# Second attention: the scores of four heads as one job of four 32-row tiles, in place of two jobs of two heads

## What is computed

```python
q = (x @ wq).reshape(b, s, 32, 8).transpose(0, 2, 1, 3)      # b = 2, s = 1024
k = (x @ wk).reshape(b, s, 8, 8).transpose(0, 2, 1, 3)
v = (x @ wv).reshape(b, s, 8, 8).transpose(0, 2, 1, 3)
q, k = rope(q), rope(k)
k, v = repeat(k, 4, axis=1), repeat(v, 4, axis=1)
scores = einsum('bhqd,bhkd->bhqk', q, k) / 8 ** 0.5
scores = where(causal, scores, -inf)
out = einsum('bhqk,bhkd->bhqd', softmax(scores), v)
x = x + layernorm(out.transpose(0, 2, 1, 3).reshape(b, s, 256) @ wo)
```

## Time and profile before

| | |
|---|---|
| median of 3 runs | 1905.16 us (1902.91 to 1907.54) |
| the profiled execution | 1904.82 us, its span 1903.1 us |
| TensorE, VectorE, ScalarE, GpSimd busy | 87%, 73%, 59%, 35% of the span |
| second attention, unit 0's first score job to the end of unit 15 | 1214.1 to 1700.7 us |
| mean granted clock of TensorE | 0.948 of full speed |

### The profile page before, as it was taken

How to read it: one execution, slowest core, us unless ns; L and a number is a source line. 1 busy time by engine, 2 the same in 40 slices (tenths; PEclk the granted TensorE clock), 3 DMA queues, 4 the chain that set the end, 5 groups by cost and what they waited for, 6 DMA issues and landing times. The chain is left out here.

```text
span 1903.1 us, 43770 instructions
## 1 busy us (share of the span) xinstructions
PE 1654.3 (87%) x14612; PEld 1020.7 (54%) x14612; DVE 1383.8 (73%) x2882; ACT 1129.0 (59%) x2158; POOL 667.5 (35%) x756
## 2 busy tenths in 40 slices
PE   3899999999999999999827745899999999982997
PEld 1577777777777777777713422233333333341554
DVE  4487777778777777777766564888888888837564
ACT  4566666666666666666545641266666666666444
POOL 0654554555455555545221123021212222223011
PEclk9899999999999999999968967899999999995998
DMA  4322111112111111211000010000000000001000
GB/s 130 88 54 49 41 47 43 43 41 52 47 41 47 44 41 41 52 47 34 17 0 1 1 36 9 17 13 15 15 13 16 12 18 11 8 1 66 1 23 22
DMA packets 53107, 61.83 MB, mean 32 GB/s; under 512 B 11345, under 2 KB 32018, under 8 KB 53010
## 3 DMA queue, kind: packets, MB, share of 16 engines
q1 hardware_dynamic: 53010, 60.55, 13.1%
HBM read 18.57 MB, written 2.10 MB: 11 GB/s over the span
## 5 line engine op out<-in xcount | busy, mean ns | idle before, releaser
L1566 ACT ACTIVATE a_prob<-psum 128x1024 f32<-128x1024 f32 (+3 forms) x384 | 302.3, 813 | 212.1 <-PE psum L1523 209.5
L1606 DVE TENSOR_REDUCE a_mx<-psum 128x1 f32<-128x512 f32 (+3 forms) x608 | 367.5, 655 | 61.2 <-PE psum L1505 55.0
L1598 POOL TENSOR_SCALAR_AFFINE_SELECT a_prob<-a_prob 128x256 f32<-128x256 f32 x256 | 103.8, 406 | 420.5 <-ACT a_prob L1566 418.0
L1502 PE MATMUL psum<-a_kd,a_qp 128*128 128x512 f16 (+3 forms) x768 | 217.5, 337 | 34.2 <-DMA a_kd<-a_k_part 22.6
L528 POOL TENSOR_TENSOR a_swp<-a_swp,a_sin 128x512 f32<-128x512 f32 x128 | 163.1, 1274 | 161.6 <-DMA a_swp<-a_lin 161.6
L884 DVE TENSOR_REDUCE a_nmax<-psum 128x1 f32<-128x1024 f32 (+7 forms) x256 | 191.3, 748 | 1.0 <-PE psum L599 1.0
L532 POOL TENSOR_TENSOR a_rope<-a_swp,a_cosd 128x512 f32<-128x512 f32 x128 | 164.2, 1283 | 12.4 <-POOL a_swp L528 4.7
L224 POOL TENSOR_TENSOR x<-x,y (+1 forms) x64 | 54.4, 879 | 319.5 <-ACT y L196 319.5
L1544 PE MATMUL psum<-a_prob,a_vg 128*32 128x512 f32 (+3 forms) x1536 | 165.4, 503 | 0.8 <-ACT a_o_sb L1572 0.4
L1502 PEld LDWEIGHTS psum<-a_kd,a_qp 128*128 128x128 f16 x768 | 70.7, 98 | 173.3 <-DVE a_mx L1606 94.4
L756 ACT ACTIVATE a_prob_big<-psum,a_nmax 128x1024 f32<-128x1024 f32 (+3 forms) x128 | 121.8, 952 | 68.5 <-DVE a_nmax L884 65.1
(11 more groups left out here) (256 smaller groups left out, 4477.8 us busy)
## 6 DMA issues: line engine op xcount, KB each, us to landing
a_swp<-a_lin SPq DMA_DIRECT2D x256, 128.0 KB, 2.3
a_qp<-a_q_part SPq DMA_DIRECT2D x192, 16.0 KB
a_kd<-a_k_part SPq DMA_DIRECT2D x192, 16.0 KB
x<-_attn_hidden_states_dram SPq DMA_DIRECT2D x4, 512.0 KB, 5.5
a_w_raw<-in_L_attn_Wq_dram SPq DMA_DIRECT2D x16, 128.0 KB, 2.3
a_w_raw<-in_L_attn_Wk_dram SPq DMA_DIRECT2D x16, 128.0 KB, 2.3
a_w_raw<-in_L_attn_Wv_dram SPq DMA_DIRECT2D x16, 128.0 KB, 2.3
a_wo_raw<-in_L_attn_Wo_dram SPq DMA_DIRECT2D x1, 2048.0 KB
```

What stands on the lines that cost most here:

```text
L1502: last = pe.matmul(to[:, j * n:(j + 1) * n], qp[:, w % 3, t * P:(t + 1) * P], kd[:, w % 3, j0 + j, a:e], start=True, stop=not edge)
L1566: act.activation(prob_at(u, i)[:, 2 * pair:2 * pair + 2, a % BANK:a % BANK + e - a], c.psum[:, pair_of(u, i):pair_of(u, i) + 2, 0:e - a], ...
L1606: dve.tensor_reduce(mx[:, t, j0:j0 + per, a // BANK], work(("S", w, i))[:, 0:per * (e - a)].rearrange("p (j n) -> p j n", j=per), AX.X, AL ...
```

## The change

A place is one score job of four heads. Its four matmuls go to four different 32-row tiles and to banks 0, 1, 2 and 3; the exponential is one instruction over four banks, up to 2048 columns; the mask is one instruction over four heads. Since there are no other four banks, a score job waits for the exponential of the job just before it. The context of a place stands directly behind the next score job. Score jobs are due at 2i + 1. ScalarE's copy of bank 4 stands one place after the half's last context place (at place 4 and at place 0 of the next unit). Scans, maxima, outputs, and VectorE's work keep their numbers and due times.

```diff
@@ the places and the order
-                KQ += [(t, max(t * P, half * BANK), (half + 1) * BANK, pair) for pair in range(2)]
-        NS, NJ, NC = len(QK), len(KQ), len(KQ) // 2
+                KQ.append((t, max(t * P, half * BANK), (half + 1) * BANK))
+        NS, NC = len(QK), len(KQ)
-            timed = [(i + 0.5, "X", i) for i in range(NJ)] if u >= 0 else []
+            timed = [(2 * i + 1, "X", i) for i in range(NC)] if u >= 0 else []
-                timed += [(2 * LAST_OF[0] + 1 + LAG + 2.6, "O", 0)]
+                timed += [(2 * LAST_OF[0] + 5.6, "O", 0)]
@@ TensorE
-                        wait(pe, exp_done, NJ * u + i - 1)
+                        wait(pe, exp_done, NC * u + i)
                         pe.wait_ge(qf_ready, 2 * u + a // BANK + 1)
-                        for h in range(2):
-                            rows = slice((2 * pair + h) * R, (2 * pair + h + 1) * R)
-                            last = pe.matmul(c.psum[:, pair_of(u, i) + h, 0:e - a], kd[rows, u % 3, 2 * pair + h, kt * P:(kt + 1) * P],
+                        for j in range(J):
+                            rows = slice(j * R, (j + 1) * R)
+                            last = pe.matmul(c.psum[:, j, 0:e - a], kd[rows, u % 3, j, kt * P:(kt + 1) * P],
                                              qf[rows, u % 2, a:e], start=True, stop=True)
@@ the context behind a score job
-                            done = NJ * u + i - LAG
-                            if done >= 0 and done % 2 == 1:
-                                context(done // NJ, done % NJ // 2)
+                            if NC * u + i >= 1:
+                                context(*divmod(NC * u + i - 1, NC))
@@ ScalarE
-                        act.activation(prob_at(u, i)[:, 2 * pair:2 * pair + 2, a % BANK:a % BANK + e - a],
-                                       c.psum[:, pair_of(u, i):pair_of(u, i) + 2, 0:e - a], ACT.Exp, scale=SCALE).then_inc(exp_done, 1)
+                        act.activation(prob_at(u, i)[:, :, a % BANK:a % BANK + e - a],
+                                       c.psum[:, 0:J, 0:e - a], ACT.Exp, scale=SCALE).then_inc(exp_done, 1)
-                            if i == 2 * LAST_OF[0] + 1 + LAG:
+                            if i == LAST_OF[0] + 1:
                                 output(u, 0)
-                            if i == LAG - 1 and u >= 1:
+                            if i == 0 and u >= 1:
                                 output(u - 1, 1)
@@ GpSimd
-                                block_ = prob_at(u, i)[:, 2 * pair:2 * pair + 2, a % BANK:a % BANK + P]
+                                block_ = prob_at(u, i)[:, :, a % BANK:a % BANK + P]
-                                                   base=0, pattern=[[0, 2], [1, P]], channel_multiplier=-1).then_inc(masked, 1)
+                                                   base=0, pattern=[[0, J], [1, P]], channel_multiplier=-1).then_inc(masked, 1)
```

More of the change, by code:

```diff
@@ L1445, in n_diagonal @@
         def n_diagonal(u, i):
-            per = [diagonal(n) for n in range(NJ)]
+            per = [diagonal(n) for n in range(NC)]
             return u * sum(per) + sum(per[:i + 1])
@@ L1468, in prob_at @@
             def prob_at(u, i):
-                return prob[:, (NC * u + i // 2) % 4, :, :]
+                return prob[:, (NC * u + i) % 4, :, :]
             with nc.Block() as block:
@@ L1535, in context @@
                     def context(u, n):
[L1536 to L1539, removed]
+                        kt, a, e = KQ[n]
+                        pe.wait_ge(exp_done, NC * u + n + 1)
+                        if diagonal(n):
+                            pe.wait_ge(masked, n_diagonal(u, n))
                         if kt == 0:
@@ L1551, in _ @@
                         if kind == "X":
-                            done = NJ * u + i - LAG
-                            if done >= 0 and done % 2 == 1:
-                                context(done // NJ, done % NJ // 2)
-                            if u == NU - 1 and i == NJ - 1:
-                                for n in range((NJ - LAG) // 2, NC):
-                                    context(u, n)
+                            if NC * u + i >= 1:
+                                context(*divmod(NC * u + i - 1, NC))
+                            if u == NU - 1 and i == NC - 1:
+                                context(u, i)
                 @block.scalar
@@ L1590, in _ @@
                     for u in range(NU):
-                        for i in range(NJ):
-                            if i == 6 and u + 1 < NU:
+                        for i in range(NC):
+                            if i == 3 and u + 1 < NU:
                                 values(u + 1)
                             if diagonal(i):
-                                kt, a, e, pair = KQ[i]
-                                pool.wait_ge(exp_done, NJ * u + i + 1)
-                                block_ = prob_at(u, i)[:, 2 * pair:2 * pair + 2, a % BANK:a % BANK + P]
+                                kt, a, e = KQ[i]
+                                pool.wait_ge(exp_done, NC * u + i + 1)
+                                block_ = prob_at(u, i)[:, :, a % BANK:a % BANK + P]
                                 pool.affine_select(out=block_, in_=block_, compare_op=ALU.is_ge, fill=0.0,
-                                                   base=0, pattern=[[0, 2], [1, P]], channel_multiplier=-1).then_inc(masked, 1)
+                                                   base=0, pattern=[[0, J], [1, P]], channel_multiplier=-1).then_inc(masked, 1)
                 @block.vector
@@ L1620, in maxima @@
                         dve.wait_ge(m_made, 2 * w + half + 1)
-                        wait(dve, x_made, NJ * (w - 1))
+                        wait(dve, x_made, NC * (w - 1))
                         dve.tensor_tensor(qf[:, w % 2, cols], work(("M", w, half)), qp[:, w % 3, cols], ALU.add).then_inc(qf_ready, 1)
```

17 lines of the change are left out of this document (7 added, 10 removed).

## The result

| | before | changed |
|---|---|---|
| median (lowest to highest), 4 runs each | 1904.05 us (1902.91 to 1907.54) | 1932.76 us (1932.22 to 1934.95) |
| ratio of the times, 95% interval | | 1.015 (1.0132 to 1.0167) |
| span of the profiled execution | 1903.1 us | 1930.5 us (time 1932.22) |
| a middle unit, first score job to first score job | 30.64 us | 32.34 us |

The change makes the kernel 28.7 us slower. The forecast was 1926 us in a range of 1909 to 1946.

The account below looks back on a forecast made before the run. TensorE's list, walked in order, was taken to set the pace, VectorE close behind. Fifteen units gave +17.9 us, unit 15 +2.8 and unit 0 +0.3: +21.0 on 1904.8, forecast 1926 us, range 1909 to 1946.

Parts of the forecast that it names:

- Relief: TensorE's list, each unit: twelve fewer score jobs save 3.2 us and changes of tile shape 0.9, together 4.1 us less.
- the much slower rival: TensorE's four score tiles don't run together, or masks take 0.81 us and more: 1946 us and beyond; chance 0.08.
- The exponential's loop: Score job to score job, waiting for the exponential directly before: at least 2.38 us at 512 columns, 0.93 at 128.
- The mask: GpSimd's mask of four heads: 0.63 us taken, between 0.41 and 0.81; the context behind the next score job waits for it.
- twice as dear: Upper end of the cost of GpSimd's four-head mask: 0.81 us, giving +29 us in all.
- The waits: TensorE's waits per unit, 6.8 us: 1.1 for exponentials, 1.1 for masks, 0.2 for ScalarE's copy, 4.5 for VectorE.
- the 5.6 that I had named as a sign of being wrong: The prediction called itself wrong if TensorE's waits stay under 5.6 us per unit.
- Middle units: Each unit grows by 1.2 us: 4.1 less work against waits rising from 1.5 to 6.8; 15 units give +17.9.
- Unit 0: The first unit starts two scans later, +0.3 us, besides the +1.2 of each unit.
- Unit 15: The last unit, without scans beside it, takes 26.8 us to its end against 24.0 laid out for before: +2.8.
- Faster: Rival: TensorE's relief comes through, waits grow by less than 4.1 us per unit, 1860 or any time under 1901; chance 0.06.
- Unchanged: Rival: relief and waits cancel at about 4.1 us per unit, needing free masks and quicker handovers; 1905 +- 4, chance 0.08.

Follow-up runs that it names:

- The kernel with both repairs: Changed kernel with contexts two places behind their score jobs instead of one and the two-input maximum as a one-input reduction; 1902.32 us, ratio 0.9994 to the kernel before.

## Why the prediction was right

**Relief, -4.1 us per unit: held.** Twelve fewer score jobs, the next start 0.32 behind four matmuls. The Trainium skill's figure of 3.07 for four row tiles ("TensorE: Matmul & The Clock Gate", Part 3, Packing small matmuls) would have made each job 0.06 longer, 0.38 us instead of 0.32; the trace doesn't show it, and where they differ the trace decides. That the 1933 us worked out from it lie beside the 1932.8 measured is chance. Neither did two-by-two tiles come, which carried most of the much slower rival. The 0.9 us for changes of tile shape in the 4.1 weren't measured by themselves; the distances below bear them out only as part of the whole.

**The exponential's loop: held.** 2.38 us at 512 columns, four times a unit, as laid out from the row by shape of pairs. Exponentials over four banks, by shape (two of the four):

```profile
L1560 ACT ACTIVATE a_prob<-psum 128x2048 f32<-128x2048 f32 x96 | 180.2, 1878 | 160.4 <-PE psum L1520 160.1
...
L1560 ACT ACTIVATE a_prob<-psum 128x512 f32<-128x512 f32 x32 | 19.1, 598 | 34.9 <-PE psum L1520 34.9
```

1.878 for 1.89 predicted, and 0.598 for 0.60. These rows are a fixed part and a slope, also across banks. The fixed cost that twelve fewer exponentials save is 12 x 0.169, 2.0 us and not the "some 1 us" of the prediction; it is off the path and changes nothing.

**The mask: held**, 0.634 for 0.63. The bound "twice as dear" wasn't needed.

**The waits, 6.8 us per unit: right in the distances but for one term, open in the split.** The rows give the idle time as 0.8 for score jobs (0.7 of it for exponentials, where I had 1.1), 1.2 for contexts (1.0 for masks and 0.2 for the copy, I had 1.1 and 0.2), 1.6 for scans and 1.2 for the maxima job (I had 4.5 for VectorE), 4.8 us. Taken as it stands this is under the 5.6 that I had named as a sign of being wrong. But the rows count from a matmul's end and my layout from the moment at which the next could have started, some 0.1 to 0.2 us earlier each time; so the rows aren't to be compared with 6.8 one by one. The distances are, and eleven of twelve hold; counted by them TensorE's waits are the 1.5 laid out for before, the 4.1 of relief and the 1.7 by which the unit grew, 7.3 us. That sum takes the 4.1 as given, so how much of the waits is VectorE's isn't shown apart. What my layout lacked is the hold on the two-input maximum: I moved GpSimd's masks and asked only who waits for them, not who runs beside them. It is 0.43 us per unit and, by the one-input kernel, 6.2 us in all (4.6 by the ratios). The Trainium skill ("SBUF — State Buffer", Who interferes with whom) has it: VectorE's second port pair is shared with GpSimd as an exclusive lock. The trace agrees (0.18 and 0.61 us), as does the kernel in which that operation is a reduction of one input (0.17).

**Middle units, +1.2: it was +1.70,** +1.27 without the hold. **Unit 0: +1.5 predicted (the +1.2 of each unit and 0.3), -1.2 measured:** the clock was at half for 3.4 us, 2.2 of them in the unit, and not for 10 as in the earlier trace rows. I had taken the drop as it was. That it was shorter is not the change's doing: the kernel before with the one-input maximum has the old order, its clock was at half for 6.8 us there, and its unit 0 took 30.38 us instead of 32.96. Its windows of unit 0, of the stretch at half clock, and of unit 15:

```profile
1215.30:1245.68 30.38, 29.88 (x222) 10.62 (x222) 25.84 (x50) 19.39 (x25) 6.28 (x16) 0.94 0.03 6
1211.88:1218.70 6.82, 5.44 (x30) 2.76 (x30) 5.22 (x11) 1.85 (x2) 0.41 (x1) 0.50 0.13 24
1673.84:1697.93 24.09, 19.14 (x178) 5.73 (x174) 1.64 (x6) 19.65 (x28) 6.95 (x18) 1.00 0.01 2
```

Beside those 30.38 us the changed kernel's 31.77 are +1.4, near the +1.5. So the -1.2 is luck.

**Unit 15: +2.8 predicted, +4.6 measured.** The 24.0 laid out for the old order are right at full clock (24.09 in the last line above). In the profiled execution of the kernel before the clock was at half for 3.4 us of this unit and it took 25.3. In the changed kernel it was at half for 3.4 us from 1699.6 and again from 1720.11 to 1730.35. The second fall came behind a stretch from 1696.59 to 1719.50 in which TensorE was busy for 14.68 of 22.91 us:

```profile
1720.11 1.51 PE L1541 MATMUL psum<-a_prob,a_vg 128*32 128x384 f32 x8 [0.51 <-POOL a_prob L1592]
```

This context took 0.85 us at full clock above. I had put 2 us for one more fall into the range and not the sum. No run has the changed kernel without such falls, so that the clock is all of the 3.1 us over the 26.8 laid out fits but isn't shown.

Part by part, measured less predicted: units 1 to 14 +7.1 (23.8 against 16.7), of which the hold is 6.0; unit 0 -2.7; unit 15 +1.8; ahead of unit 0 -1.4; behind unit 15 +1.6. That is 6.4 us of span, 27.4 against 21.0.

Ahead of unit 0 nothing was changed, and over all the profiled kernels the first score job starts anywhere from 1212.0 to 1215.3. Behind unit 15 the clock stayed at half for another 3.9 us; in the four other profiled executions in which it did so for 3.0 to 5.2 us, 203.4 to 205.1 us follow unit 15, and 202.4 to 202.9 in the seven in which it didn't (204.0 and 202.4 in the changed kernel and the one before). So the term that I missed is as large as the whole error, and the others nearly cancel, the clock having a part in most of them: that the total came within 7 us is in part luck.

**The rivals.** Faster: its condition was waits that grow by less than 4.1 us per unit, and they grew by 5.8 (1.70 + 4.1). Unchanged: it wanted free masks and quicker handovers; with free masks the kernel still stood at 1914, and its waits had grown by 4.7 (0.58 + 4.1) where 4.6 were laid out. The kernel with both repairs shows what the relief is worth without mask waits and hold: 1902 us, next to nothing. That is what the rule cited with this rival gives (the Trainium skill, "TensorEngine Tiling (Array Packing)", PSUM Bottleneck), for a kernel which the change was not; the waits came on top.

## What to carry to other kernels

A relief of the busiest engine is worth what the next one leaves of it: 1.8 us per unit brought 0.8 here, and the merge's 4.1 brought 0.3 even with the mask waits and the hold repaired, and cost 1.7 with them. When work moves on an engine, list what now runs beside it as well as who waits for it; an instruction that has one length all through the kernel and another one in a single place (0.18 and 0.61 us), ending with an instruction of another engine, may well be held by it, and another form of the same work tells. And look at how evenly an order feeds the second engine before changing what the first one does: spacing by width, together with later contexts, gained about 1% with either form of the score job.

## What was unexpected of the hardware

- A VectorE maximum of two inputs of 4 numbers per partition in SBUF takes 0.18 us alone, 0.38 beside a 0.41 us mask on GpSimd and 0.61 beside one of 0.63; as a reduction with one input 0.17 beside the same mask. A cast of one input of 4 numbers takes 0.18 alone and 0.32 when it starts 0.11 us into a mask of 0.41.
- Two masks of 128x256 directly behind each other take 0.77 us, not 2 x 0.406; one of 128x512 takes 0.634.
- Four matmuls in four 32-row tiles, 512 columns each, let the next matmul start after 0.32 us, as two do.
- The clock at unit 0 was at half for 10 us before and 3.4 us after the change, and for 6.8 us in a kernel with the old order, though nothing in the work ahead of it was changed; what moves it isn't settled. With the old order, 10 us or 6.8 of it made 32.96 or 30.38 us of unit 0.
